# Reordering two attentions and giving a routed expert stage its own ring buffers, on one core

## The reference

```
x = x + latent cross-attention(ctx, layernorm(x))   # 16 heads of 64; keys: 512 rows of x and 32 of ctx
x = x + top-1 experts(layernorm(x))                 # 8 experts: silu(a)*g @ w2, hidden 512, router has a bias
x = x + attention(layernorm(x), keys = ctx)         # 16 heads of 8, one shared key/value head of 32 rows
x = x + top-2 experts(layernorm(x))                 # 8 experts, hidden 256, router without bias
```

## Time and profile before

| | |
|---|---|
| median of 3 runs | 970.61 us (969.95 to 977.39) |
| the profiled execution | 967.55 us |
| its span, first to last instruction | 965.8 us |
| PE busy | 831.6 us, 86% |
| DVE busy | 463.9 us, 48% |
| ACT busy | 379.0 us, 39% |
| POOL busy | 303.7 us, 31% |
| mean granted TensorE clock | 0.902 of full |

### The profile page before, as it was taken

One profiled execution on the slowest core, in us unless ns is written; L12 is line 12 of the kernel. 1 busy time (PEld: TensorE's weight loads), 2 busy tenths in 40 slices (PEclk: granted clock), 3 DMA queues, 4 the chain that ended last, 5 costly groups with the idle time before them and its releaser, 6 DMA issues.

```text
span 965.8 us, 14568 instructions
## 1 busy us (share of the span) xinstructions
PE 831.6 (86%) x4851; PEld 479.5 (50%) x4851; DVE 463.9 (48%) x1160; ACT 379.0 (39%) x598; POOL 303.7 (31%) x340
## 2 busy tenths in 40 slices
PE   5899999999999999999999999339993888519891
PEld 4544455455455445456445454336662466515550
DVE  4535463564553664553473561334443145336552
ACT  4464544454443454443534442103332424103330
POOL 5133222322321522321432323131334005544441
PEclk9999999999999999998999999658996667559996
DMA  9999996000000000000110000301116000112225
GB/s 215 148 151 151 152 150 142 2 1 1 1 1 1 12 2 1 1 1 1 60 40 1 1 1 6 93 18 33 45 34 180 6 1 24 33 48 58 70 62 144
DMA packets 75632, 50.48 MB, mean 52 GB/s; under 512 B 3910, under 2 KB 72394, under 8 KB 75562
## 3 DMA queue, kind: packets, MB, share of 16 engines
q1 hardware_dynamic: 72042, 42.29, 26.0%
q0 software_dynamic: 3520, 7.27, 2.3%
HBM read 20.07 MB, written 29.47 MB: 51 GB/s over the span
## 4 chain that ended last, share of the span: by engine, by line
PE 76%; DVE 6%; DMA 5%; ACT 5%; issue 5%; POOL 2%; SPq 1%; DVEq 0%; POOLq 0%; ACTq 0%
PE PSUM L1340 16%; PE PSUM L1358 13%; PE PSUM L1311 6%; PE PSUM L1470 6%; PE PSUM L1398 4%; PE PSUM L1224 3%; PE PSUM L1228 3%; PE PSUM L1376 3%; PE PSUM L1490 3%; PE PSUM L1362 3%; PE PSUM L1230 3%; PE PSUM L1229 2%; PE PSUM L1559 2%; DMA PT<-lists_d 2%; PE PSUM L1318 2%
## 5 line engine op out<-in xcount | busy, mean ns | idle before, releaser
L589 POOL TENSOR_TENSOR PSUMS<-PT 128x1024 f32<-128x1024 f32 x64 | 151.2, 2363 | 406.6 <-ACT PT L720 183.1
L720 ACT ACTIVATE PT<-PSUM 128x1024 f32<-128x1024 f32 x128 | 131.0, 1024 | 259.2 <-PE PSUM L1340 258.8
L996 DVE TENSOR_REDUCE TOPS<-PSUM 128x2 f32<-128x544 f32 x256 | 175.1, 718 | 80.4 <-PE PSUM L1311 75.2
L1358 PE MATMUL PSUM<-PT,BIG 128*64 128x512 f32 x512 | 137.4, 617 | 0.4 <-ACT OT L733 0.4
L1311 PEld LDWEIGHTS PSUM<-KH,QH 64*128 64x128 f32 x512 | 42.8, 188 | 106.4 <-DVE TOPS L996 49.1
L1470 PE MATMUL PSUM<-BIG,PT 128*128 x170 | 87.4, 619 | 0.0
L1311 PE MATMUL PSUM<-KH,QH 64*128 64x272 f32 x512 | 74.0, 345 | 3.0 <-DVE KL L989 1.7
L1119 DVE TENSOR_TENSOR PSUMS<-PSUMS,PSUM 128x256 f32<-128x256 f32 (+1 forms) x62 | 32.2, 520 | 69.3 <-ACT PSUMS L770 69.3
L1340 PE MATMUL PSUM<-TOPROW,MINUS 64*128 64x512 f32 x320 | 64.5, 389 | 0.1
L770 ACT ACTIVATE PSUMS<-PSUM 128x256 f32<-128x256 f32 (+1 forms) x62 | 28.7, 463 | 84.8 <-PE PSUM L1470 84.8
L1340 PE MATMUL PSUM<-QH,KH 64*128 64x512 f32 x256 | 58.0, 444 | 0.8 <-ACT VC L684 0.8
(11 more groups left out here) (241 smaller groups left out, 1394.0 us busy)
## 6 DMA issues: line engine op xcount, KB each, us to landing
lists_d<-EMPTY SPq DMA_DIRECT2D x3, 2730.0 KB, 47.2
lists_b<-EMPTY SPq DMA_DIRECT2D x3, 2470.0 KB, 42.9
BIG<-in_L_ffn_w SPq DMA_DIRECT2D x2, 2048.0 KB, 9.7
lists_d<-EMPTY SPq DMA_DIRECT2D x1, 2665.0 KB, 44.8
PT<-lists_d SPq DMA_DIRECT2D x39, 65.0 KB, 1.9
lists_b<-EMPTY SPq DMA_DIRECT2D x1, 2405.0 KB, 20.5
BIG<-in_L_ffn_w SPq DMA_DIRECT2D x4, 512.0 KB, 6.4
PT<-results_d SPq DMA_DIRECT2D x8, 256.0 KB, 5.3
```

The lines of the kernel that those rows point to most:

```text
L589: pool.tensor_tensor(PSUMS[:, kt // 2], PTT[:, i % 2, kt - 1], PTT[:, i % 2, kt], ALU.add).then_inc(s_ps, 1)
L720: act.activation(PTT[:, i % 2, kt], PSUM[:, place:place + 2, :], ACT.Exp, scale=DH ** -0.5).then_inc(s_exp, 1)
L996: dve.tensor_reduce(TOPS[:, c // 2, c % 2, :], PSUM[:, place:place + 2, 0:HALF], AX.X, ALU.max).then_inc(s_max, 1)
L1358: last = pe.matmul(dst, V[:, b % 2, kt, cols], PTT[:, i % 2, kt, h, :], start=kt == 0, stop=False)
```

## The change

1. First attention: `pv(0)` and `pv(1)` stand together, `rows` comes after `scores(2)`, the `top` parts are dealt out anew, and what is in `at_d` comes before `pv(4)` instead of after it.
2. The bias of the first router is added by DVE as it copies the logits; the four bias matmuls are gone. The bias is loaded into all partitions.
3. Second attention: `order_c` is written out by hand. Each batch starts on its scores earlier, and the `feat` and `q` steps of later batches stand where earlier batches take exponentials. `r_rest` comes before `c_proj`. `c_pv` goes over the four groups of heads on the outside and begins when the first half of the exponentials is there. `c_oturn` uses bank 6 instead of 7.
4. The two slots of the second routing are made by three DVE operations instead of six, and one copy of the reciprocal is dropped.
5. Rings: `XG`, `XGT`, `SIL`, `HIDT`, `YS`, the tables and `W2ALL` get places of their own, over buffers that only the first attention's projections use. `YS` has 8 places, ring numbers run on through both expert stages, and a fetch waits only for DVE's scaling, no longer for the scatter. `w1` is loaded as a gate half and an up half, `w2` as soon as the last queries, keys and values are made. One register load per tile goes.

The core of the diff:

```
-            order += scores(1) + at_a + pv(0)
+            order += scores(1) + at_a + pv(0) + pv(1) + top(0, 1)
+            order += scores(2) + top(2)
             if i:
                 order.append(("rows", i - 1))
-            order += top(0, 1) + pv(1) + top(2, 3) + pv(2) + top(4)
-            order += scores(2) + top(5) + pv(3) + top(6, 7)
+            order += top(3, 4) + pv(2) + top(5, 6) + pv(3) + top(7)
             order += scores(3) + scores(4)
             if i + 1 < ALL:
                 order.append(("max_turn", i + 1))
-            order += at_b + at_c + pv(4) + at_d
+            order += at_b + at_c + at_d + pv(4)
...
-        order_c = [(name, b) for _, b, name in sorted((at + (3 if at < 10 else 12) * b, b, name) for b in range(B) for name, at in STEPS_C)]
+        order_c = [(step.rstrip("0123"), int(step[-1])) for step in (
+            "c_stats0 c_scale0 c_norm0 c_feat0 c_stats1 c_scale1 c_q0 c_stats2 c_norm1 c_top0 c_feat1 c_topturn0 "
+            "c_scores0 c_stats3 c_q1 c_scale2 c_pv0 c_top1 c_norm2 c_feat2 c_oturn0 c_scale3 c_topturn1 c_proj0 "
+            "c_scores1 c_q2 r_stats0 c_pv1 r_scale0 c_norm3 r_norm0 c_top2 r_turn0 c_oturn1 r_logits0 r_hot0 "
+            "c_topturn2 r_rest0 c_proj1 c_feat3 r_stats1 c_scores2 r_run0 r_scale1 r_norm1 r_slot0 c_q3 c_pv2 c_top3 "
+            "r_turn1 c_oturn2 r_logits1 c_topturn3 r_hot1 r_front0 r_rest1 c_proj2 r_back0 r_stats2 c_scores3 r_run1 "
+            "r_slot1 r_scale2 c_pv3 r_front1 r_norm2 r_back1 r_turn2 r_logits2 c_oturn3 r_hot2 r_rest2 c_proj3 "
+            "r_stats3 r_run2 r_scale3 r_norm3 r_turn3 r_slot2 r_front2 r_back2 r_logits3 r_hot3 r_rest3 r_run3 "
+            "r_slot3 r_front3 r_back3").split()]
...
-            sp.dma_start(RB[0:1, :], rb.rearrange("(a e) -> a e", a=1)).then_inc(ld_r, 16)
+            sp.dma_start(RB[:, :], rb.rearrange("(a e) -> a e", a=1).broadcast_to([P, E])).then_inc(ld_r, 16)
...
-                    if j >= 8:
+                    if before + j >= 8:
 
                         sp.wait_ge(s_ysc, before + j - 7)
-                        sp.wait_ge(*scattered(which, j - 8))
...
-                    tell(dve.tensor_copy(L, by_tile))
+                    if which == 0:
+                        dve.wait_ge(ld_r, 48)
+                        tell(dve.tensor_tensor(L, by_tile, RBT, ALU.add))
+                    else:
+                        tell(dve.tensor_copy(L, by_tile))
...
-                    dve.wait_ge(s_dn, before + j + 1)
-                    if before + j >= 4:
-                        dve.wait_ge(*(scattered(which, j - 4) if j >= 4 else scattered(0, max(
-                            i for i in range(TILES_B) if i % 4 == j % 4))))
-                    dve.tensor_scalar(YS[:, j % 4, :], PSUM[:, 6, 0:D], XG[:, j % 8, D + 1:D + 2], None, ALU.mult).then_inc(s_ysc, 1)
+                    g = before + j
+                    dve.wait_ge(s_dn, g + 1)
+                    if g >= 8:
+                        dve.wait_ge(*scattered(g - 8))
+                    dve.tensor_scalar(YS[:, g % 8, :], PSUM[:, 6, 0:D], XG[:, g % 8, D + 1:D + 2], None, ALU.mult).then_inc(s_ysc, 1)
...
-                        dst = PSUM[:, place, t * E:(t + 1) * E]
-                        pe.matmul(dst, XT[:, t * P:(t + 1) * P], RW[:, 0, :], start=True, stop=False)
-                        last = pe.matmul(dst, ONES[0:1, :], RB[0:1, :], start=False, stop=True)
+                        last = pe.matmul(PSUM[:, place, t * E:(t + 1) * E], XT[:, t * P:(t + 1) * P], RW[:, 0, :],
+                                         start=True, stop=True)
...
-                    pe.wait_ge(*CPA[a].at(0, "exp1"))
                     pe.wait_ge(s_vb, 2 * (a + 1))
                     claim(4, 5)
-                    for t in range(TPB):
-                        for c in range(4):
+                    for c in range(4):
+                        if c % 2 == 0:
+                            pe.wait_ge(*CPA[a].at(0, f"exp{c // 2}"))
+                        for t in range(TPB):
...
-                    turned(7, lambda t: ON[:, a % 2, t * P:(t + 1) * P], TPB, CPP[a].sem)
-                    free[7] = CPA[a].at(0, "kept")
+                    turned(6, lambda t: ON[:, a % 2, t * P:(t + 1) * P], TPB, CPP[a].sem)
+                    free[6] = CPA[a].at(0, "kept")
```

More of the change, by code:

```diff
@@ L550, in scale_and_bias, with send @@
                 pool.tensor_tensor(NMR[:, j, 0:n], NMR[:, j, 0:n], RSTD[:, j, 0:n], ALU.mult).then_inc(made.sem, 1)
-            def send(which, b, steps, run, rows):
-                pool.wait_ge(cleared[which], 64)
-                for k in range(which + 1):
-                    pool.wait_ge(*steps.at(run, f"slot{k}" if which else "wt0"))
-                    for t in range(TPB):
-                        pool.indirect_dma_start(
-                            LIST[which], bass.IndirectOffsetOnAxis(ap=SLOT[:, b % 2, k, t:t + 1].bitcast(U32), axis=0),
-                            rows[k][:, t, :], None).then_inc(s_sent[which][b % 2], 16)
+            def send(which, b, rows, parts):
+                for k, t in parts:
+                    pool.indirect_dma_start(
+                        LIST[which], bass.IndirectOffsetOnAxis(ap=SLOT[:, b % 2, k, t:t + 1].bitcast(U32), axis=0),
+                        rows[k][:, t, :], None).then_inc(s_sent[which][b % 2], 16)
             def experts(which):
@@ L578, in pool_program @@
                 elif name == "r0_send":
[L579 removed]
+                    pool.wait_ge(cleared[0], 64)
+                    pool.wait_ge(*RD0.at(a, "wt0"))
+                    send(0, a, [NRM], [(0, t) for t in range(TPB)])
                 elif name == "scores" and a[1] in (1, 3):
@@ L893, in route @@
                 L, tmp, hot, hot2, L2, ex = (ROUT[:, b % 2, i] for i in range(6))
-                top, top2, tmp2, sm, rc, rc2, place_f = (RSM[:, b % 2, i] for i in range(7))
-                place, share = PLACE[:, b % 2, 0], PLACE[:, b % 2, 1]
+                top, top2, tmp2, sm, rc, rc2 = (RSM[:, b % 2, i] for i in range(6))
+                place_f = RSM[:, b % 2, 6:7 + which]
+                place, share = PLACE[:, b % 2, 0], PLACE[:, b % 2, 1:2 + which]
                 def after(name):
@@ L1468, in gate_up @@
                         claim(bank + 1)
-                    for n in range(2 * FF // BANK):
-                        last = pe.matmul(PSUM[:, bank + n, :], XGT[:, j % 3, :], weights1[:, n * BANK:][:, bass.ds(at1[j], BANK)],
+                    for n, weights in enumerate((W1G, W1U) if which == 0 else (WGUALL,)):
+                        last = pe.matmul(PSUM[:, bank + n, :], XGT[:, (before + j) % 3, :], weights[:, bass.ds(at[j], BANK)],
                                          start=True, stop=True)
-                    read_columns(j + 1, j)
+                    read_columns(j + 1)
                     last.then_inc(s_gu, 1)
@@ L1489, in down @@
                     for f in range(NF):
-                        last = pe.matmul(PSUM[:, 6, 0:D], HIDT[:, j % 2, f * P:(f + 1) * P],
-                                         weights2[:, f * D:][:, bass.ds(at2[j], D)], start=f == 0, stop=f == NF - 1)
+                        last = pe.matmul(PSUM[:, 6, 0:D], HIDT[:, (before + j) % 2, f * P:(f + 1) * P],
+                                         weights[:, f * D:][:, bass.ds(at[j], D)], start=f == 0, stop=f == NF - 1)
                     last.then_inc(s_dn, 1)
```

243 lines of the change are left out of this document (117 added, 126 removed).

## The result

The changed kernel takes 928.9 us (median of four runs, 925.1 to 931.5) where the kernel before takes 970.3: the ratio is 0.956, with a 95% interval of 0.949 to 0.962. The forecast was 939.5, so the direction was right and 10.6 us of gain were missed; the stated range ended at 930. The profiled execution went from 967.55 to 926.59.

A forecast was written before the change was run, and what follows sets the result against it. PE's work bounds the first attention and stage B, chains through all engines the second attention, and scatter-delayed fetches slow stage D. Gains of 16.9, 2.4, 8.9 and 2.9 sum to 31.1 us: 970.61 to 939.5, range 930 to 953.

The forecast's parts named there:

- part 1, order of the loop: First attention's loop: fewer changes of PE's array shape save 6.7 us, less 1 us for small waits.
- bias and clock drops, in the loop: First attention's loop: fewer bias matmuls save 4.4 us, and three low-clock stretches behind the logits vanish, saving 6.8 us.
- end of the first attention: Last batch's router logits after the loop: without bias matmuls, 2.4 us less on the path at the lower clock.
- part 3, second attention: Second attention and routing: fewer exponential waits 5 us, later batches' steps moved 2.5, earlier statistics 1.4; together 8.9 us.
- part 4, stage D: Second expert stage: fetches no longer wait for scatters, so 1.942 us a tile becomes 1.865; 2.9 us saved.
- the second term of part 3: Second attention, first maxima to first sums: later batches' steps move into PE's short waits, saving 2.5 us.
- the 1.4 us for the statistics: Second routing, last batch: DVE does statistics right behind its addition, without batch 2's remaining routing between; 1.4 us.
- Halves: Second attention: `c_pv` starts on the first half of exponentials, with a later `c_q` before it; saves 5 of 6.1 us.
- No stretch under 1.00: First attention's loop: sign of a right forecast, PE's clock never below full between 30 and 600 us.
- the rival that went by the page, 946: First attention's loop: low-clock stretches have another cause and stay, 6.8 us less gain, 946 us; chance 0.20.
- the slower rival: First attention's loop: `top(4)` waits for the exponential of `scores(2)` in 31 turns, undoing the gain; chance 0.02.
- The rival of 933: Second attention: PE waits less and holds 2.4 GHz longer, giving 6 us more, 933 us; chance 0.10.

The follow-up runs named there:

- e3: Changed kernel with the old order of steps in the loop of the first attention; 923.5 us, 0.954 of the kernel before.
- e7: Kernel before with only the bias change, DVE adding the bias instead of PE; 956.0 us, 0.984 of the kernel before.
- e5: Changed kernel run again without an edit; 924.6 us, 0.954 of the kernel before.
- e4: Changed kernel with SP waiting before each fetch for the scatter of the tile eight before; 927.3 us, 0.958 of the kernel before.
- e12: Changed kernel with `r_rest` of a batch put behind the next batch's `c_proj`; 933.2 us, 0.961 of the kernel before.
- e8: Changed kernel with the second attention's steps up to the first `c_pv` in the old list's order; 934.4 us, 0.964 of the kernel before.
- f2: Changed kernel with its new list up to the first `c_pv`, most later steps in old relative order; 940.5 us, 0.968 of the kernel before.
- e6: Changed kernel with `c_pv` waiting for both halves of the exponentials before its first matmul; 932.0 us, 0.963 of the kernel before.
- e11: Changed kernel with 50 unread matmuls on PE ahead of the first tiles of stages B and D; 933.3 us, 0.961 of the kernel before.
- f4: f3 plus unread matmuls filling PE's three long waits (28, 50 and 60); 921.8 us, 0.950 of the kernel before.
- e10: Changed kernel with 118 unread matmuls on PE in the second attention, 68 of them within the batches' chain; 934.4 us, 0.964 of the kernel before.
- f3: Changed kernel with stage B's tables before the head mask's sum and old loop order in eight reciprocal turns; 928.8 us, 0.955 of the kernel before.

## Right and wrong, step by step

| term | forecast | measured | by |
|---|---|---|---|
| part 1, order of the loop | 5.7 | 2.7 | e3 against the changed kernel |
| bias and clock drops, in the loop | 11.2 | 11.2 to 11.35 | e7, e3 against before |
| end of the first attention | 2.4 | 3.0 | table above |
| part 3, second attention | 8.9 | 22.9; 15.9 with the stop | e5; first profile |
| part 4, stage D | 2.9 | 5.4 | e4 against e5 |
| start | 0 | 2.4, by chance | e5, e12 |
| stage B | 0 | 0.7, not explained | table above |

**The step that failed** is the second term of part 3: the `c_feat` and `c_q` between the first maxima and the first sums "are not saved but moved to where PE waited", priced at 2.5 us. In e8 these steps, put back with the norms that they read, cost 11.7 us of C and 9.8 of the time. I counted PE's work, and the waits of the last batch's sums; but PE takes its queue in order, and each of these steps waited for its own ACT result while the scores behind it were ready. The first batch takes 8.2 us from reduction to sums in the changed kernel, 14.5 with these steps put back (733.72 to 748.23 in e8), and 15.9 before. The sums of the last batch start 68.8 us behind the last scatter of B in e5 and 86.9 before, 18.1 earlier, where I had 7.5, and from there to the last sends it takes 27.2 us instead of 32.0, where I had 1.4. The rows, before and then e5:

```profile
818.02 6.83 PE L1559 MATMUL PSUM<-PTC,PT 128*128 128x36 f32 x32 [1.50 <-ACT PT L797]
```

```profile
784.68 3.73 PE L1574 MATMUL PSUM<-PTC,PT 128*128 128x36 f32 x32 [0.33 <-ACT PT L811]
```

My upper bound of 14, "no waits", was drawn from the same view of one batch and was too low. The order of all the other steps of the list had no term but the 1.4 us for the statistics; it is worth 13.7 us of C with the old front and 2 to 6 with the new one (f2).

**Halves.** I gave them 5 us with the `c_q` in between; e6 prices the halves alone at 5.3 in C. Right in size. The 1.4 us for the statistics are seen as an order in the rows (0.73 us from addition to statistics in place of 2.12), but moving `r_rest` back cost nothing that e12 shows.

**Clock in the loop.** Right in the main: the drops behind the logits follow the sixteen small matmuls, five times out of six, and never the eight. "No stretch under 1.00" holds for the first profile's loop, up to 589.4, but in six of the others there is one, which costs about 1.5 us. The Trainium skill (TensorE: Matmul & The Clock Gate, Part 1) ties the fall to an idle stretch. At the edges of the stages e11 and f4 agree with it: low when PE had been idle, full where it worked through. The three drops in the loop came without recorded idle time, and there the measurement decides: the rival that went by the page, 946, did not come. The later drop in six profiles has 0.79 us of idle PE before it, but so have eight profiles without it.

**Part 1.** The gains of a turn were right, 0.15 and some 0.3; the count was wrong. My 31 turns held those in which DVE's reciprocals are ahead of the `top` reductions, and these got longer by 0.12 to 0.30, where I had allowed "a little more". `top(4)` waiting for its exponential, the slower rival, did not come.

**Part 4.** The mechanism was right and the size too small: 1.865 us a tile, from one stretch that I took for undisturbed, is 1.815 without the wait.

**Clock in the second attention.** The rival of 933 lies nearest to the result, but not for its reason. The mean clock is 0.65 after and 0.61 before, and e10, which raised it to 0.86 with idle matmuls, was no faster.

## What to carry to other kernels

In a queue that runs in order, look for each step's own wait and count it against the first thing ready behind it, batch by batch, not only at the last batch. Here work of a later batch, put into another's round trip while its own input was not ready, cost 11.7 us. Before such a time is compared over a few us, run the same program on another chip.

## What was not expected

The stop, above. Also that idle matmuls on PE can shorten a kernel: 138 of them, all in long waits and lasting to their ends, went with 7 us less (f3 to f4, a part of it perhaps the shorter stop); 50 that ended 1.65 and 4.35 us before the work gave none.
